# Embedding lookups by one-hot matmul: ids cast to floats ahead of the compare, and the third layer issued behind the next lookup

## What is computed

```python
e = jnp.stack([tbl_0[ids[:, 0]], ..., tbl_26[ids[:, 26]]], axis=1)
z = jnp.einsum('bfd,bgd->bfg', e, e)[:, tril_i, tril_j]      # 351 pairs, k=-1
h = jnp.concatenate([z, dense_ctx], axis=1)                  # 351 + 16
h = jnp.maximum(h @ W_top1 + b_top1, 0.0)                    # 512
h = jnp.maximum(h @ W_top2 + b_top2, 0.0)                    # 256
y = h @ W_top3                                               # 1
```

## Time and profile before

| | us |
|---|---|
| median of 3 runs | 420.1 (419.85 to 423.21) |
| the profiled execution | 421.49 |
| its span | 419.6 |
| PE (matmuls) busy | 366.5 |
| VectorE (DVE) busy | 302.3 |
| GpSimd (POOL) busy | 275.4 |
| ScalarE (ACT) busy | 210.4 |

### The profile page before, as it was taken

The page is one execution under the profiler, slowest core; times in us unless marked ns, Lnnn a source line. Parts: engine busy times, 40 slices in busy tenths (PEclk is TensorE's granted clock), DMA queues, the critical chain, the costliest instruction groups (busy, mean ns, idle before and its releaser), DMA issues.

```text
span 419.6 us, 14576 instructions
## 1 busy us (share of the span) xinstructions
PE 366.5 (87%) x6180; PEld 323.4 (77%) x6180; DVE 302.3 (72%) x996; ACT 210.4 (50%) x435; POOL 275.4 (66%) x286
## 2 busy tenths in 40 slices
PE   0858669899898999999899998899899998999788
PEld 0757559898698878898698977888688986998565
DVE  2999968993689837995589936996479935891320
ACT  3446263745435482635526573634617463564822
POOL 4777777777777778777777778777775777400020
PEclk9999969999899999999899999999999998999989
DMA  7974362242232423233232422223231421100000
GB/s 276 339 229 143 90 209 77 60 123 66 70 85 58 135 57 84 57 89 105 77 84 58 134 59 84 59 65 126 68 93 36 116 54 51 41 10 5 5 10 5
DMA packets 19601, 37.70 MB, mean 90 GB/s; under 512 B 6792, under 2 KB 8400, under 8 KB 19536
## 3 DMA queue, kind: packets, MB, share of 16 engines
q0 software_dynamic: 8896, 17.89, 16.4%
q1 hardware_dynamic: 8704, 16.00, 11.5%
q10 hardware_dynamic: 1936, 2.89, 2.1%
HBM read 35.88 MB, written 0.01 MB: 86 GB/s over the span
## 4 chain that ended last, share of the span: by engine, by line
PE 39%; DVE 36%; ACT 16%; issue 6%; DMA 3%; SPq 1%; ACTq 0%; DVEq 0%
DVE one_hot L633 29%; PE fill_ps L430 9%; PE mlp_ps L460 9%; PE pair_ps L447 8%; PE fill_ps L431 8%; ACT et L540 7%; ACT work L330 6%; DVE work L330 5%; DMA work<-tbl_d 3%; PE fill_ps L413 1%; PE fill_ps L475 1%; DVE table_lo L620 1%; PE mlp_ps L493 1%; PE mlp_ps L486 1%; ACT table_hi L533 1%
## 5 line engine op out<-in xcount | busy, mean ns | idle before, releaser
L391 POOL DMA_INDIRECT rows<-tbl_d,ids_sb x272 | 271.4, 998 | 89.8 <-issue 80.8
L633 DVE TENSOR_SCALAR one_hot<-hot_ids,chunk_row 128x256 fp32r<-128x256 int32 x720 | 220.3, 381 | 3.2 <-PE fill_ps L431 2.5
L430 PE MATMUL fill_ps<-one_hot,table_hi 128*128 128x256 f32 x720 | 191.5, 302 | 27.2 <-DVE one_hot L633 25.3
L431 PE MATMUL fill_ps<-one_hot,table_lo 128*128 128x256 f32 x720 | 183.2, 290 | 0.0
L430 PEld LDWEIGHTS fill_ps<-one_hot,table_hi 128*128 128x128 f32 x720 | 143.2, 199 | 40.4 <-issue 21.7
L431 PEld LDWEIGHTS fill_ps<-one_hot,table_lo 128*128 128x128 f32 x720 | 143.7, 200 | 0.0
L330 DVE COPY work<-pair_ps 26x112 f32<-26x112 f32 (+1 forms) x256 | 66.1, 258 | 66.4 <-PE pair_ps L447 63.2
L330 ACT COPY work<-pair_ps 26x112 f32<-26x112 f32 (+1 forms) x256 | 60.9, 238 | 94.4 <-PE pair_ps L447 91.7
L540 ACT COPY et<-fill_ps 128x512 f32<-128x512 f32 (+1 forms) x80 | 78.0, 1100 | 0.4
L552 ACT COPY et<-fill_ps 128x512 f32<-128x512 f32 x40 | 46.4, 1213 | 60.2 <-PE fill_ps L431 51.0
L447 PE MATMUL pair_ps<-et 128*26 128x26 f32 x4096 | 52.9, 193 | 9.8 <-issue 5.5
(11 more groups left out here) (21 smaller groups left out, 60.3 us busy)
## 6 DMA issues: line engine op xcount, KB each, us to landing
hot_ids<-ids_hot_d SPq DMA_DIRECT2D x34, 256.0 KB, 3.9
rows<-tbl_d,ids_sb POOLq DMA_INDIRECT x272
work<-tbl_d SPq DMA_DIRECT2D x4, 640.0 KB, 4.1
work<-tbl_d SPq DMA_DIRECT2D x4, 512.0 KB, 7.4
hot_ids<-ids_hot_d ACTq DMA_DIRECT2D x6, 256.0 KB, 7.3
w_sb<-w_d ACTq DMA_DIRECT2D x1, 768.0 KB
w_sb<-tbl_d SPq DMA_DIRECT2D x1, 640.0 KB, 4.2
w_sb<-tbl_d SPq DMA_DIRECT2D x1, 512.0 KB, 12.1
```

Source lines behind the costliest of these rows:

```text
L391: nc.gpsimd.indirect_dma_start(out=rows[:, t, c, :], out_offset=None, in_=tables[f], in_offset=bass.IndirectOffsetOnAxis(ap=ids_sb[:, tile ...
L430: nc.tensor.matmul(to, table_hi[:, CHUNK_AT[k] + c, :], hot, start=(c == 0), stop=False)
L431: last = nc.tensor.matmul(to, table_lo[:, CHUNK_AT[k] + c, :], hot, start=False, stop=(c == CHUNKS_OF[k] - 1))
L633: last = nc.vector.tensor_scalar(one_hot[:, (first + c - c0) % ONE_HOT_RING, :], hot_ids[:, slot, (k - k0) * COLS:(k - k0 + 1) * COLS], ch ...
```

## The change

Layer 3 of a group is taken from the end of the block and put behind the first lookup of the next block; the last but one goes between the last two pair banks. ScalarE gets a new function `cast_ids`, which turns the ids of a lookup step from int32 into floats in place (a copy of 128x512), two lookup steps ahead; the first two casts stand ahead of its first table cast. VectorE's compare reads the ids as floats and waits for the cast in place of the DMA. `chunk_row`, the column of row numbers, was of type float before.

```diff
--- before.py
+++ after.py
@@ -85,10 +85,11 @@
             steps += hot[:3] + cold[0] + hot[3:] + [("pairs", g, 0)] + cold[1][:2] + [("pairs", g, 1)] + cold[1][2:]
         else:
             b = g - 1
-            steps += [hot[0], ("pairs", b, 2), hot[1], ("pairs", b, 3), hot[2]] + cold[0][:2] + [hot[3]] + cold[0][2:4]
+            steps += [hot[0]] + ([("layer3", b - 1)] if b > 0 else [])
+            steps += [("pairs", b, 2), hot[1], ("pairs", b, 3), hot[2]] + cold[0][:2] + [hot[3]] + cold[0][2:4]
             steps += hot[4:] + cold[0][4:] + [("layer1", b), ("pairs", g, 0)] + cold[1][:2]
-            steps += [("layer2", b, 0), ("pairs", g, 1)] + cold[1][2:] + [("layer2", b, 1), ("layer3", b)]
-    return steps + [("pairs", GROUPS - 1, 2), ("pairs", GROUPS - 1, 3)]
+            steps += [("layer2", b, 0), ("pairs", g, 1)] + cold[1][2:] + [("layer2", b, 1)]
+    return steps + [("pairs", GROUPS - 1, 2), ("layer3", GROUPS - 2), ("pairs", GROUPS - 1, 3)]
 
 
 STEPS = order()
@@ -263,6 +264,7 @@
         consts = sem("consts")
         ident_ok = sem("ident_ok")
         chunk_row_ok = sem("chunk_row_ok")
+        hot_ids_float = sem("hot_ids_float")
         cold_full = sem("cold_full")
         fill_moved = sem("fill_moved")
         pair_full = sem("pair_full")
@@ -533,6 +535,14 @@
                 nc.scalar.copy(table_hi[:, CHUNK_AT[k]:CHUNK_AT[k] + CHUNKS_OF[k], :],
                                raw_table(k)).then_inc(hi_made, 1)
 
+            def cast_ids(step):
+
+                _, g, j = step
+                slot, n = HOT_FILL[step] % IDS_RING, hot_fills(g)[j][1]
+                ids = hot_ids[:, slot, 0:n * COLS]
+                act.wait_ge(hot_ids_in[slot], 16 * (HOT_FILL[step] // IDS_RING + 1))
+                nc.scalar.copy(ids.bitcast(F32), ids).then_inc(hot_ids_float, 1)
+
             def move_cold(step):
                 _, g, t, j = step
                 c0, n = cold_fills(g)[j]
@@ -573,10 +583,15 @@
                 move_pairs(act, g, bank, (2, 3), pair_moved_a, nc.scalar.copy)
 
             early = []
+            fills = list(HOT_FILL)
+            for step in fills[:2]:
+                cast_ids(step)
             for k in range(4):
                 make_high(k)
             for step in STEPS:
                 if step[0] == "hot":
+                    if HOT_FILL[step] + 2 < len(fills):
+                        cast_ids(fills[HOT_FILL[step] + 2])
                     if step[1] == 0:
                         for k in range(2 * step[2] + 4, min(2 * step[2] + 6, MOST_HOT)):
                             make_high(k)
@@ -624,14 +639,14 @@
 
                 slot = HOT_FILL[step] % IDS_RING
                 k0 = hot_fills(step[1])[step[2]][0]
+                ids = hot_ids[:, slot, (k - k0) * COLS:(k - k0 + 1) * COLS].bitcast(F32)
                 at = sum(WIDTHS[:WIDTHS.index(CHUNKS_OF[k])])
-                dve.wait_ge(hot_ids_in[slot], 16 * (HOT_FILL[step] // IDS_RING + 1))
+                dve.wait_ge(hot_ids_float, HOT_FILL[step] + 1)
                 for half, (c0, c1) in enumerate(halves(k)):
                     part, first = PARTS[step, k, half]
                     wait_count(dve, hot_used, parts_in_the_way(first + c1 - c0))
                     for c in range(c0, c1):
-                        last = nc.vector.tensor_scalar(one_hot[:, (first + c - c0) % ONE_HOT_RING, :],
-                                                       hot_ids[:, slot, (k - k0) * COLS:(k - k0 + 1) * COLS],
+                        last = nc.vector.tensor_scalar(one_hot[:, (first + c - c0) % ONE_HOT_RING, :], ids,
                                                        chunk_row[:, at + c:at + c + 1], None, ALU.is_equal)
                     last.then_inc(hot_made, 1)
```

## The result

The changed kernel takes 404.9 us (403.43 to 407.34 in four runs) against 420.9 us for the one before on the same chip: a ratio of 0.962, with a 95% interval of 0.955 to 0.969. The prediction was 401.6 us, inside a range of 391 to 410. The profiled execution took 403.43 us with a span of 401.5, so its span is 18.1 us shorter than that of before; the sum had said 18.5. The median fell by 16.0. A ratio in this document leaves out executions that were slower as a whole at a lower clock, so it can differ a little from the quotient of two medians.

What follows compares the result with a forecast made beforehand. A ring of layer 2, layer 3, first lookup, pair bank, VectorE's chain and layer 1 was taken to bound each block. Terms of -12.0, -6.9 and +0.4 gave -18.5 us: 403.0 profiled, 401.6 as median, range 391 to 410.

Steps and rivals of the forecast that it cites:

- The sum: Whole kernel: -12.0 - 6.9 + 0.4 = -18.5 us, profiled execution from 421.5 to 403.0 us.
- Part 1: Layer 3 behind the next lookup: pair bank starts 2.0 us earlier in each of six blocks, 12.0 us.
- The seventh layer 3: Layer 3 in the tail: gains 0, bounds 0.4 us either way; its pair bank waits for the last cold fill.
- Part 2: First lookups after the stop at layer 3: four falls to a lower clock go, 1.7 us each, 6.9 us.
- Part 3: ScalarE casting ids: 40 copies of about 0.62 us, covered in the blocks; start 0.4 us later, bounds 0 to 1.2.
- Part 4: VectorE's one-hot compares from floats: 0 ns change each, bounds 60 ns less and 20 ns more.
- A: Layer 3 pays but the clock still falls as often: 408.5 us; chance 0.12.
- B: Floats shorten VectorE's compare until TensorE's matmuls bound its stretch, 2.4 us a block: 392 us half, 384 full effect; chance 0.18.
- C: Float compares shut GpSimd out more and its gathers become the bound: slower, over 500 us in all; chance 0.05.
- D: VectorE or ScalarE takes back layer 3's gain through a late cast or copy of y: 416 to 422; chance 0.06.

Runs made afterwards that it cites:

- The order alone: Layer 3 moved behind the next lookup in the kernel before, no casts, compares from integers; run alone 404.3 us against 419.6, ratio 0.964.
- the kernel kept busy at the stop: Kernel before, old order, with four unused matmuls put into TensorE's stop at layer 3; run alone 419.4 us against 420.8, ratio 0.998.
- the casts and floats alone: Changed kernel with layer 3 put back in its old place; run alone 421.8 us against 420.3 for the kernel before, ratio 1.003.
- the compare sizes: Kernel before with 36 unused compares at its end, 128, 256 and 512 columns, integers and floats: 425.9 us against 418.5, one execution each.
- the version that beats both: Layer 3 moved, no casts, integer compares; in pair banks 2 and 3 VectorE moves one strip, ScalarE three; alone 394.9 us against 420.3, ratio 0.941.

## Why the prediction was right, point by point

- **The sum.** The profiled execution agrees with the sum to 0.4 us, and that is partly luck: the start was 0.6 us worse than forecast and the tail 0.7 us better, and the six blocks gave 18.3 us for 18.9. Against the median, 404.9, the forecast of 401.6 is 3.3 us too low.
- **Part 1, layer 3.** Named 2.0 us for each of six blocks, 12.0 in all. The table gives 2.13 and 12.8 as it stands, and 1.98 and 11.9 with the kinds of first move matched. The mechanism stood step by step: the lookup follows layer 2 at once, VectorE begins its next one-hots at 153.36 without waiting for y, and it waits 0.2 us at most for layer 3. The order alone gave the whole ratio.
- **The seventh layer 3.** Taken as 0 with bounds of 0.4; the tail was 0.74 us shorter, outside these bounds. In the profiled execution of before 2.06 us of its pair banks went to waiting for instructions and are missing after, so this term was not separated further.
- **Part 2, the clock.** In the profiled execution all falls in the six blocks went, as forecast. The forecast priced the four at 1.7 us each, 6.9 in all. The price measured is 1.4 us from the table as it stands, 1.6 with the first moves matched, and 1.6 to 1.9 by the copies of y against the kernel kept busy at the stop. So 1.7 stands as well as these measures can tell. The kernel kept busy also confirmed the link, but it lost in its tail what it had won, so the median did not show the gain. The executions still differ after the change: two of the four took 403.4 and 403.6 with a granted clock of 0.987, two 406.3 and 407.3 with 0.983. The profiled one is the fastest of the four, which goes with its 18.1 us against 16.0 for the median.
- **Part 3, the casts.** Estimated at 0.62 us, measured 0.66 on average. They were covered in the blocks: the casts and floats alone left the time where it was, 1.003 (1.000 to 1.007). At the start 0.4 us was forecast; it was 0.3 where the floats stood alone. In the changed kernel's profile the table's own DMA was later and hid it, and VectorE's first moves came 0.96 us later, inside the bounds of 0 to 1.2.
- **Part 4, the floats.** Taken as 0 ns, shown as 0 at three widths. The rule of the Trainium skill ("VectorE: DVE Perf Modes", What auto-detection actually checks), by which the type is no condition of the 2-port mode, agrees with this case: the slope is 134 ns for 256 columns with both types. A clean look at the slope would have been a stronger ground than the 263 against 267 ns of the prediction, which differ by little.
- **Rivals.** A (falls as often) did not come in the profiled execution. B fell with the compare sizes. C did not come, and the opposite did (last section). D did not come. The half of B that was right is its bound: once VectorE's stretch was shortened in another way, the period did go down to TensorE's, by 1.5 us and not 2.4.

## What to carry to other kernels

When an in-order engine waits for a late result that only a side branch needs, issue the side branch one step of ready work later. Look at every other engine that stands in the same place in the shared order: here VectorE stood in front of its next one-hots until y was there, and came along with the move. Before feeding an engine another type to make it faster, measure the two types at three widths with nothing else running; one profile answers it. And after a bound is moved, read the chain again: one strip given to the idle engine was worth another 2.4% (0.941 for 0.964).

## What the runs showed of the hardware that was not expected

**GpSimd's long gathers went with the stop.** Before, the longest gather took 4,867 ns, and six took 1.7 to 4.9 us, each beginning near a copy of y. After, the longest is at the start:

```profile
L393 POOL DMA_INDIRECT rows<-tbl_d,ids_sb x272: 940/944/1568, 5.9 to 347.7; - x136
```

In the old order the wait for y let VectorE's one-hots run back to back behind it, 263 ns apart, and these shut the gather out. In the run from 170.19 the 56 are about 312 ns apart, and the gathers keep 944 ns. With floats alone the old order had gathers of 4.8 us again, and so had the kernel kept busy at the stop. How long the gather lasted went with TensorE's clock. At the 12 stops of these three profiled executions behind which the clock stayed up it took 4.6 to 4.9 us, and at the six where the clock fell 1.4 to 2.8 us. What decides whether GpSimd gets its turn was not isolated. The gathers had time to spare, so it cost nothing here.

The gathers in turn go with slower one-hots. After the change the last 40 begin at 350.02, when the last gather, begun at 347.7, is over:

```profile
350.02 10.61 DVE L649 TENSOR_SCALAR one_hot<-hot_ids,chunk_row 128x256 fp32r<-128x256 f32 x40
```

They take 10.61 us, 263 ns apart. In the kernel kept busy they begin at 359.49, gathers go on to 369.7, and they take 12.32 us. With the strip given to ScalarE they begin at 337.10, gathers go on to 347.3, and it is 12.33 us. So one-hots made while gathers run took some 50 ns more each.

**TensorE can run short of instructions.** In the two sets with several kernels the small pair matmuls, 128 records to a bank, waited for their own instructions, and the clock granted was 0.79 to 0.86. The waits in the second set's run of the order alone:

```profile
PEld pair_ps L448 <- issue: 185.8, 214, 2.6
PE pair_ps L448 <- issue: 161.9, 192, 2.6
```

Before it was 5.5 us in two goes for the same line. The same kernels run alone were at their usual times again, one of them on a chip that had also served such a set. What slowed the supply is open. Under it the order alone was slower than the kernel before (1.083), and the version that beats both was 1.021, so their gains are not safe where instructions are short.
